# Squared key norms read from the gram's diagonal through DRAM, with every engine's list reordered

## Chip, cores and metric

One core of a Trainium2 chip runs the kernel. The metric is device time in microseconds (us) of one execution; a median over several executions is compared. TensorE (PE), VectorE (DVE), ScalarE (ACT), GpSimd (POOL) and SyncE (SP) each work through a list of their own, in order. SP only issues DMAs. "PEld" is PE's weight load and "SPq" is SP's queue of issues.

## What is computed

The input x is [8, 2048, 256]. The layer is attention with a gated delta rule, a layer norm, a feed-forward network (FFN) and a last layer norm. Cut to what matters:

```python
x_act = tanh(x); static_out = x_act @ W.T            # keys = queries = x_act, 16 heads of 16
# per head and token:  S = lam*S; u = beta*(v - S^T k); S += k u^T; o = S^T q
y = static_out + o
x1 = layernorm(x + layernorm(y)*gamma + ln_beta)
out = layernorm(x1 + (silu(x1 Wg^T) * (x1 Wu^T)) Wd^T)
```

As query and key are the same vector, the output of a token holds u times the key's squared norm. That norm, per token and head, is what the change touches.

## The kernel before

The sequence is cut into 32 steps of T = 64 tokens for all 8 batches, and a step into 4 windows of 16 tokens. A 128-row tile holds 8 batches x 16 tokens. Within a window the recurrence is solved in closed form. The state passes from window to window, so four such chains follow one another in each step and the steps follow each other. One window's chain is: PE `pe_keys_by_state` (keys times state), DVE and ACT form the rest R (`dve_rest_high`, `dve_rest_sum`, `act_rest`, `dve_rest_low`), PE `pe_inverse_by_rest` (the inverse of the window's triangular system times R), DVE and ACT form U (`act_update`, `dve_update_high`, `dve_update_low`), PE `pe_keys_by_update`, DVE and ACT form the new state S (`dve_state_high`, `dve_state_sum`, `act_state`, `dve_state_low`). All three products are L182.

Around it, software-pipelined by hand-written lists (`pe_step`, `dve_step`, `act_step`, `pool_step`, `sp_step`, one call of each per step; `live(s + k)` says for which neighbouring step a piece is done):

- Two steps ahead: SP loads x (`sp_load_x`, L994), ACT takes tanh of it in place in xa (L677), PE transposes the keys (L239), ACT and DVE split them into two float16 parts xt (L691, L406), SP stores xt to DRAM (`sp_store_keys`, L1003) and spreads it back to the block-diagonal e and the packed xb (L1016, L1025, 8 DMAs each).
- One step ahead: PE makes the gram matrices (`pe_gram`, L216), ACT and DVE add them up in gs (L715, L434), SP stores gs to DRAM and loads it back as gh with a (head, batch) pair in each partition (`sp_store_gram` L1033, `sp_load_gram` L1040), DVE multiplies by nmask (`dve_mask_gram`, L428), ACT copies it to tt (L721), and DVE inverts it in 28 operations (L443, L451). SP stores the inverse and loads tb (L1047, L1059), and loads kb, the keys as weights (L1072, 8 DMAs for each half step). A kb half may be loaded only when the window before that reads it last has ended (`sp` semaphore). PE's static output is L227 (`pe_static_out`).
- Norms: when k16 and the transposes have read xa, ACT squares it in place (`act_square`, L682) and DVE sums 16 columns each into nb (`dve_square_sums`, L418). The next x may be loaded only after that (`nr`). `dve_key_norms` (L423) scales nb, and POOL multiplies U by it (`pool_attention_out`, L915).
- Two steps behind: gate and up matmuls (L253), silu (L777), multiply (L495), split (L783, L953), down matmuls (L279), norms (L749, L757, L763) and the store.

SP waits at the head of a helper and then issues that helper's DMAs. Whatever stands behind a wait in its list is held up too.

Of the kernel before, what the change touches and what calls it, by code (L numbers as in the profile page):

```python
# [12 lines left out]
P = 128  # L13
# [3 lines left out]
NW = 4  # L17
# [18 lines left out]
def build(nc, x, W, ln_gamma, ln_beta, eta, lam_logit, w_gate, w_up, w_down, out):  # L36
# [3 lines left out]
    with ctx:  # L40
# [3 lines left out]
        def sem(name):  # L44
# [24 lines left out]
        nb = sb("nb", [P, 2, NW, H])  # L69
# [49 lines left out]
        scr_g = nc.dram_tensor("scr_g", [H, B, C, T], F32).ap()  # L119
        scr_t = nc.dram_tensor("scr_t", [2, H, B, C, T], F16).ap()  # L120
# [3 lines left out]
            sq=1, nr=1, nb=1, k16h=2, k16=2,  # L124
# [36 lines left out]
        FIRST, LAST = -3, NS + 3  # L161
# [122 lines left out]
        def pe_step(pe, s, p):  # L284
            if live(s - 2):
                pe_gate(pe, s - 2, p, 0)
                pe_up(pe, s - 2, p, 0)
                pe_gate(pe, s - 2, p, 1)
                pe_up(pe, s - 2, p, 1)
                pe_gate(pe, s - 2, p, 2)  # L290
                pe_up(pe, s - 2, p, 2)
                pe_gate(pe, s - 2, p, 3)
            if live(s):
                pe_keys_by_state(pe, s, p, 0)
            if live(s - 2):
                pe_gate(pe, s - 2, p, 4)
                pe_up(pe, s - 2, p, 3)
                pe_up(pe, s - 2, p, 4)
            if live(s + 1):
                pe_gram(pe, s + 1, 1 - p, 0, range(0, 8))  # L300
                pe_gram(pe, s + 1, 1 - p, 0, range(8, 16))
                pe_gram(pe, s + 1, 1 - p, 1, range(0, 8))
                pe_gram(pe, s + 1, 1 - p, 1, range(8, 16))
            if live(s - 2):
                pe_gate(pe, s - 2, p, 5)
            if live(s + 1):
                pe_gram(pe, s + 1, 1 - p, 2, range(0, 8))
                pe_gram(pe, s + 1, 1 - p, 2, range(8, 16))
            if live(s - 2):
                pe_up(pe, s - 2, p, 5)  # L310
                pe_down(pe, s - 2, p, 0, range(0, 4))
            if live(s + 1):
                pe_gram(pe, s + 1, 1 - p, 3, range(0, 8))
            if live(s):
                pe_inverse_by_rest(pe, s, p, 0)
            if live(s + 1):
                pe_gram(pe, s + 1, 1 - p, 3, range(8, 16))
            if live(s - 2):
                pe_down(pe, s - 2, p, 0, range(4, 6))
            if live(s):  # L320
                pe_keys_by_update(pe, s, p, 0)
            if live(s - 2):
                pe_down(pe, s - 2, p, 1, range(0, 3))
                pe_down(pe, s - 2, p, 1, range(3, 6))
            if live(s):
                pe_keys_by_state(pe, s, p, 1)
            if live(s + 1):
                pe_static_out(pe, s + 1, 1 - p, 0)
            if live(s):
                pe_inverse_by_rest(pe, s, p, 1)  # L330
            if live(s + 1):
                pe_static_out(pe, s + 1, 1 - p, 1)
            if live(s):
                pe_keys_by_update(pe, s, p, 1)
            if live(s + 1):
                pe_static_out(pe, s + 1, 1 - p, 2)
            if live(s):
                pe_keys_by_state(pe, s, p, 2)
            if live(s + 1):
                pe_static_out(pe, s + 1, 1 - p, 3)  # L340
            if live(s):
                pe_inverse_by_rest(pe, s, p, 2)
                pe_keys_by_update(pe, s, p, 2)
            if later(s + 2):
                pe_transpose_keys(pe, s + 2, p, 0)
                pe_transpose_keys(pe, s + 2, p, 1)
            if live(s):
                pe_keys_by_state(pe, s, p, 3)
                pe_inverse_by_rest(pe, s, p, 3)
            if live(s - 1):  # L350
                pe_transpose_x1(pe, s - 1, 1 - p, 0)
                pe_transpose_x1(pe, s - 1, 1 - p, 1)
            if live(s):
                pe_keys_by_update(pe, s, p, 3)
# [60 lines left out]
        def dve_square_sums(dve, q, p):  # L415
            dve.wait_ge(SEM["y1"], n_of("y1", q - 2))
            dve.wait_ge(SEM["sq"], n_of("sq", q))
            dve.tensor_reduce(nb[:, p, :, :], xa[:, :, :].rearrange("p n (h k) -> p n h k", h=H),  # L418
                              AX.X, ALU.add).then_inc(SEM["nr"], 1)

        def dve_key_norms(dve, q, p):
            dve.wait_ge(SEM["nr"], n_of("nr", q))
            dve.tensor_scalar(nb[:, p, :, :], nb[:, p, :, :], sc[:, BETAR:BETAR + 1], -0.5 / RS,  # L423
                              ALU.mult, ALU.add).then_inc(SEM["nb"], 1)
# [79 lines left out]
        def dve_step(dve, s, p):  # L504
            if live(s - 1):
                dve_state_sum(dve, s - 1, 1 - p, 3)
                dve_state_low(dve, s - 1, 1 - p, 3)
                dve_statistics(dve, s - 1, 1 - p, 1)
                dve_statistics(dve, s - 1, 1 - p, 2)
            if live(s + 1):  # L510
                dve_scale_keys(dve, s + 1, 1 - p, 0)
            if live(s - 2):
                dve_multiply(dve, s - 2, p, 1)
                dve_multiply(dve, s - 2, p, 2)
            if live(s):
                dve_key_norms(dve, s, p)
                dve_store_inverse(dve, s, p, 1)
            if live(s - 1):
                dve_statistics(dve, s - 1, 1 - p, 3)
            if live(s):  # L520
                dve_rest_high(dve, s, p, 0)
            if live(s - 1):
                dve_moments(dve, s - 1, 1 - p)
            if live(s - 2):
                dve_multiply(dve, s - 2, p, 3)
            if live(s + 1):
                dve_gram(dve, s + 1, 1 - p, 0)
            if live(s):
                dve_rest_sum(dve, s, p, 0)
            if live(s - 2):  # L530
                dve_multiply(dve, s - 2, p, 4)
            if live(s + 1):
                dve_gram(dve, s + 1, 1 - p, 1)
            if live(s - 1):
                dve_load_residual(dve, s - 1, 1 - p)
            if live(s - 2):
                dve_multiply(dve, s - 2, p, 5)
            if live(s):
                dve_rest_low(dve, s, p, 0)
            if live(s + 1):  # L540
                dve_gram(dve, s + 1, 1 - p, 2)
            if live(s):
                dve_update_high(dve, s, p, 0)
                dve_update_low(dve, s, p, 0)
            if live(s + 1):
                dve_gram(dve, s + 1, 1 - p, 3)
            if live(s - 2):
                dve_add_ffn(dve, s - 2, p, 0)
                dve_add_ffn(dve, s - 2, p, 1)
            if live(s - 1):  # L550
                dve_attention_norm(dve, s - 1, 1 - p, 0)
            if live(s):
                dve_state_high(dve, s, p, 0)
            if live(s - 1):
                dve_attention_norm(dve, s - 1, 1 - p, 1)
            if live(s):
                dve_state_sum(dve, s, p, 0)
            if live(s - 1):
                dve_attention_norm(dve, s - 1, 1 - p, 2)
            if live(s):  # L560
                dve_state_low(dve, s, p, 0)
            if live(s - 1):
                dve_attention_norm(dve, s - 1, 1 - p, 3)
            if live(s + 1):
                dve_scale_keys(dve, s + 1, 1 - p, 1)
            if live(s - 2):
                dve_add_ffn(dve, s - 2, p, 2)
                dve_add_ffn(dve, s - 2, p, 3)
            if live(s):
                dve_rest_high(dve, s, p, 1)  # L570
                dve_rest_sum(dve, s, p, 1)
                dve_rest_low(dve, s, p, 1)
            if live(s + 1):
                dve_square_sums(dve, s + 1, 1 - p)
            if live(s):
                dve_update_high(dve, s, p, 1)
                dve_update_low(dve, s, p, 1)
                dve_statistics(dve, s, p, 0)
                dve_state_high(dve, s, p, 1)
                dve_state_sum(dve, s, p, 1)  # L580
                dve_state_low(dve, s, p, 1)
            if live(s + 1):
                dve_mask_gram(dve, s + 1, 1 - p)
            if live(s):
                dve_rest_high(dve, s, p, 2)
                dve_rest_sum(dve, s, p, 2)
                dve_rest_low(dve, s, p, 2)
            if live(s + 1):
                dve_invert_scale(dve, s + 1, 1 - p, 1)
# [713 lines left out]
```

## Time and profile before

| | |
|---|---|
| median of 3 runs | 1710.55 us (1705.41 to 1717.15) |
| profiled execution | 1699.24 us, span 1697.4 us |
| PE / DVE / ACT / POOL busy | 80% / 80% / 66% / 50% |
| mean granted PE clock | 0.881 |
| DMA queue of SP | 52.1% of 16 engines, 701072 packets |

The profiled execution is one run, 11 us under the median of the others. Busy shares are averages over the whole span. A steady step lasts about 49 us, and in it the engines take turns at being late.

### The profile page before, as it was taken

How to read it: one execution, taken by the hardware profiler on the slowest of the kernel's cores; microseconds unless marked ns; L12 is line 12 of the kernel's file. 1: busy time of each engine (PE TensorE's matmuls, PEld its weight loads, DVE VectorE, ACT ScalarE, POOL GpSimd, SP SyncE). 2: the span in 40 equal slices, each digit the busy share in tenths (PEclk: the TensorE clock that was granted, in tenths of full speed). 3: DMA queues.
4: the chain of work that ended last, by engine and by line, in shares of the span. 5: the costliest groups of instructions: out<-in, count | busy, mean ns of one | idle time of the engine just before them, and what ended most of it. 6: DMA issues, size and time to landing. Idle time of an engine off the chain costs nothing.

```text
span 1697.4 us, 53741 instructions
## 1 busy us (share of the span) xinstructions
PE 1362.5 (80%) x21032; PEld 1062.5 (63%) x21032; DVE 1352.3 (80%) x3461; ACT 1115.9 (66%) x2357; POOL 842.8 (50%) x1106
## 2 busy tenths in 40 slices
PE   4357888888888888888888888887888888888764
PEld 3345676666666666666666666666666666666542
DVE  5588888888888888888888888888788788888841
ACT  3335777667767776676777677766667677676544
POOL 6124455555544655454455555445555544555542
PEclk9557889989989998898899899898999899899877
DMA  4556445565655555566455566654565555455200
GB/s 121 118 109 119 106 122 121 119 124 114 130 118 120 122 122 116 114 123 130 110 120 119 120 125 117 125 116 115 115 116 121 114 131 117 118 117 120 52 23 25
DMA packets 701325, 190.98 MB, mean 113 GB/s; under 512 B 620944, under 2 KB 688528, under 8 KB 701072
## 3 DMA queue, kind: packets, MB, share of 16 engines
q1 hardware_dynamic: 701072, 187.56, 52.1%
q8 instruction: 165, 2.70, 0.7%
q14 instruction: 88, 0.72, 0.1%
HBM read 103.55 MB, written 67.11 MB: 101 GB/s over the span
## 4 chain that ended last, share of the span: by engine, by line
DVE 29%; SPq 18%; PE 16%; DMA 13%; issue 12%; ACT 8%; POOL 4%; ACTq 0%; POOLq 0%; DVEq 0%
SPq L1059 8%; DMA xa<-L_attn_x 6%; PE pc L182 6%; DMA scr_g<-gs 5%; PE pg L253 4%; DVE tt L451 4%; SPq L1072 4%; PE pu L253 4%; DVE gs L443 3%; DVE gate L495 3%; SPq L994 3%; DVE xt L406 2%; DVE x1lo L488 2%; DVE U L382 2%; DVE R L377 2%
## 5 line engine op out<-in xcount | busy, mean ns | idle before, releaser
L953 POOL TENSOR_TENSOR hlo<-gate,hhi 128x512 f16<-128x512 f32 x192 | 264.0, 1385 | 357.0 <-ACT hhi L783 354.9
L182 PE MATMUL pc<-R,tb 128*128 128x32 f16 x4096 | 158.1, 186 | 119.3 <-DVE R L372 117.3
L182 PEld LDWEIGHTS pc<-R,tb 128*128 128x128 f16 x4096 | 146.7, 118 | 139.8 <-DVE R L372 137.7
L182 PE MATMUL pc<-U,kb 128*128 128x32 f16 x4096 | 158.9, 188 | 85.3 <-DVE U L382 85.1
L182 PEld LDWEIGHTS pc<-U,kb 128*128 128x128 f16 x4096 | 146.9, 118 | 114.7 <-DVE U L382 114.6
L182 PEld LDWEIGHTS pc<-S,e 128*128 128x128 f16 x4096 | 150.1, 118 | 67.9 <-DVE S L399 64.4
L182 PE MATMUL pc<-S,e 128*128 128x32 f16 x4096 | 157.1, 186 | 41.5 <-DVE S L399 41.4
L279 PE MATMUL pd<-wd_t,hhi 128*128 128x256 f16 x768 | 174.5, 274 | 7.5 <-POOL hlo L953 5.1
L279 PE MATMUL pd<-wd_t,hlo 128*128 128x256 f16 x768 | 174.1, 274 | 0.0
L216 PEld LDWEIGHTS pf<-xb,e 128*128 128x128 f16 x4096 | 153.8, 118 | 31.5 <-DMA e<-scr_x 16.3
L216 PE MATMUL pf<-xb,e 128*128 128x32 f16 x4096 | 156.3, 191 | 17.5 <-DMA e<-scr_x 15.9
L495 DVE SCALAR_TENSOR_TENSOR gate<-pu,gate 128x512 f32<-128x512 f32 x192 | 129.0, 685 | 48.0 <-ACT gate L777 35.1
L443 DVE TENSOR_TENSOR gs<-tt,gh 128x56 f32<-128x56 f32 (+6 forms) x448 | 145.2, 324 | 23.6 <-ACT tt L721 14.6
L253 PE MATMUL pg<-x1hi,wg_t 128*128 128x512 f16 x384 | 154.2, 402 | 11.5 <-DVE x1lo L488 10.0
L777 ACT ACTIVATE gate<-pg 128x512 f32<-128x512 f32 x192 | 113.7, 593 | 75.5 <-PE pg L253 71.8
L451 DVE TENSOR_TENSOR tt<-tt,gs 128x56 f32<-128x56 f32 (+6 forms) x448 | 146.4, 327 | 12.1
L783 ACT ACTIVATE hhi<-gate 128x512 f16<-128x512 f32 x192 | 119.7, 629 | 49.8 <-DVE gate L495 48.1
L253 PE MATMUL pg<-x1lo,wg_t 128*128 128x512 f16 x384 | 152.1, 396 | 0.0
L253 PE MATMUL pu<-x1lo,wu_t 128*128 128x512 f16 x384 | 149.0, 388 | 0.0
L253 PE MATMUL pu<-x1hi,wu_t 128*128 128x512 f16 x384 | 149.0, 388 | 0.0
L227 PE MATMUL pf<-w_t,xt 128*128 128x256 f16 x1024 | 139.4, 282 | 0.4 <-DVE gs L434 0.4
L434 DVE SCALAR_TENSOR_TENSOR gs<-pf,gs 128x256 f32<-128x256 f32 x128 | 85.0, 664 | 62.2 <-ACT gs L715 62.0
(132 smaller groups left out, 3222.4 us busy)
## 6 DMA issues: line engine op xcount, KB each, us to landing
xa<-L_attn_x SPq DMA_DIRECT2D x128, 128.0 KB
scr_x<-xt SPq DMA_DIRECT2D x64, 256.0 KB, 2.1
xb<-scr_x SPq DMA_DIRECT2D x256, 64.0 KB, 2.9
e<-scr_x SPq DMA_DIRECT2D x256, 64.0 KB, 3.7
scr_g<-gs SPq DMA_DIRECT2D x32, 512.0 KB, 3.5
gh<-scr_g SPq DMA_DIRECT2D x32, 512.0 KB, 3.3
kb<-k SPq DMA_DIRECT2D x512, 32.0 KB, 2.3
scr_t<-t SPq DMA_DIRECT2D x64, 256.0 KB, 3.6
```

The source lines that it names most:

```text
L182: last = pe.matmul(pc2[:, :, cols], stationary(h, a), moving[:, :, cols], start=a == 0, stop=a == 1)
L216: last = pe.matmul(pf[n % 2][:, 2 * h * C:2 * (h + 1) * C].rearrange("p (z j) -> p z j", z=2), E[p][:, ez, h, :, :, n].rearrange("p b i -> ...
L227: last = pe.matmul(pf[g][:, (n % 2) * D:(n % 2 + 1) * D], xt[:, half, xz, :, :, n].rearrange("p b i -> p (b i)"), w_t[:, half, wz, :], sta ...
L253: last = pe.matmul(bank[:, :], wt[:, half, t * P:(t + 1) * P], xp[:, half, :], start=half + part == 0, stop=half + part == 2)
L279: last = pe.matmul(pd[:, (n % 2) * D:(n % 2 + 1) * D], hp[:, t, n * P:(n + 1) * P], wd_t[:, t, :], start=n % 2 + t + part == 0, stop=n % 2 ...
L443: dve.tensor_tensor(tmp[:, m, 0:C - 1 - j, :], tt[:, m, j:j + 1, :].to_broadcast([P, j, C - 1 - j, NW]), gh[:, i, j, :][:, None].to_broadc ...
L451: dve.tensor_tensor(tt[:, m, i, :], tt[:, m, i, :], tmp[:, m, 0:C - 1 - j, :], ALU.add)\
L495: dve.scalar_tensor_tensor(gate[:, k, :], pu[k][:, :], W_SCALE * HS / XS, gate[:, k, :], ALU.mult, ALU.mult).then_inc(SEM["h"], 1)
L777: act.activation(gate[:, k, :], pg[k][:, :], ACT.Silu, scale=W_SCALE / XS).then_inc(SEM["si"], 1)
L783: act.activation(hhi[:, t, :], gate[:, t % 2, :], ACT.Copy).then_inc(SEM["hh"], 1)
L953: pool.tensor_tensor(hlo[:, t, :], gate[:, t % 2, :], hhi[:, t, :], ALU.subtract).then_inc(SEM["hl"], 1)
L1059: sp.dma_start(tb[C * b:C * (b + 1), g, :, b].rearrange("j h i z m -> j h (i z m)"), scr_t[g, :, b].rearrange("h j t -> j h t")).then_inc( ...
```

## The change

`act_square` and `dve_square_sums` go. The diagonal of the gram is the squared norm itself. nmask gets ones on its diagonal (it had zeros), so the masked gh keeps the norms there. SP writes this diagonal to a DRAM scratch, 16 bytes at a time, and reads it back with (batch, token) in the partitions. nb has four buffers by step and the layout [P, 4, H, NW]. The next x now waits for k16 in place of the sums. The helpers that issue 8 or 4 DMAs are cut into parts, so that the lists can interleave them, and all five lists are written anew.

```diff
-            sq=1, nr=1, nb=1, k16h=2, k16=2,
+            kd=16, nr=16, nb=1, k16h=2, k16=2,
...
-        def dve_square_sums(dve, q, p):
...
-        def act_square(act, q, p):
...
+                if z == 2:
+                    act.wait_ge(SEM["va3"], n_of("va3", q - 1))
...
             sp.wait_ge(SEM["tf"], n_of("tf", q - 1))
+            sp.sem_inc(s_hop, 1)
+            sp.wait_ge(SEM["kd"], n_of("kd", q - 1))
             sp.dma_start(gh[:, :, :, :].rearrange("p i j n -> p (i j n)"),
...
+        def sp_store_norms(sp, q, p):
+            sp.wait_ge(SEM["tf"], n_of("tf", q, 1))
+            sp.sem_inc(s_hop, 1)
+            sp.wait_ge(SEM["nr"], n_of("nr", q - 1))
+            sp.dma_start(scr_n.rearrange("h b i n -> (h b) i n"),
+                         gh[:, :, :, :].rearrange("p i j n -> p (i j) n")[:, 0:C * C:C + 1, :])\
+              .then_inc(SEM["kd"], 16)
+
+        def sp_load_norms(sp, q, p):
+            sp.wait_ge(SEM["kd"], n_of("kd", q))
+            sp.sem_inc(s_hop, 1)
+            sp.wait_ge(SEM["y1"], n_of("y1", q - 4))
+            sp.dma_start(nb[:, q % 4], scr_n.rearrange("h b i n -> (b i) h n")).then_inc(SEM["nr"], 16)
...
+            link(eng.memset(flat[:, 0:C * C:C + 1], 1.0))
```

The lists are rotated and reordered. Read in cyclic order, with the offset of the step behind the name, the pieces that changed their neighbours are these. SP before, from the store of the keys of step q = 0: store_keys 0 and 1, packed (8), spread (8), store_inverse 0 of -1, residual (4), store_inverse 1, load_inverse 0 (8), kb 1 (8), store_gram, load_gram, load_inverse 1 (8), x of +1 (4), store_out (4), kb 0 (8). SP after:

```text
store_keys 0, 1;  packed 2, spread 2, packed 6, spread 6;  store_inverse 0;  residual 4;
load_inverse 0 (8);  kb 1 (4);  store_inverse 1;  kb 1 (4);  store_gram;
load_inverse 1 (4);  x (2);  load_inverse 1 (4);  load_gram;  x (2);
kb 0 (2);  STORE_NORMS;  kb 0 (2);  store_out 4;  LOAD_NORMS;  kb 0 (4)
```

- PE: `pe_up(4)` stands behind the first two grams, where it stood ahead of them. `pe_inverse_by_rest(0)` stands ahead of both halves of gram 3. Static outputs 0 and 1 both follow `pe_keys_by_state(1)`, 2 follows `pe_inverse_by_rest(1)`, 3 follows `pe_inverse_by_rest(2)`. They stood one each behind keys 1, inverse 1, update 1 and keys 2.
- DVE: `dve_scale_keys(0)` and `dve_store_inverse(1)` move into the stretch of the grams, the latter to behind gram 2. `dve_statistics(0)` and `dve_invert_scale(3)` move by one or a few places, the latter to ahead of `dve_update_low(2)`.
- ACT: `act_decay(2)` moves to behind the variances, `act_rest(3)` ahead of all four `act_first_norm`, which had two ahead of it. `act_hidden(1)` stands ahead of `act_store_inverse(0)`.
- POOL keeps its cyclic order.

## Rows read from the trace of the kernel before

**Rows 1.** The page's busy times, its chain, and the tile gh.

```profile
PE 1362.5 (80%) x21032; PEld 1062.5 (63%) x21032; DVE 1352.3 (80%) x3461; ACT 1115.9 (66%) x2357; POOL 842.8 (50%) x1106
...
DVE 29%; SPq 18%; PE 16%; DMA 13%; issue 12%; ACT 8%; POOL 4%; ACTq 0%; POOLq 0%; DVEq 0%
...
L428 DVE TENSOR_TENSOR gh<-gh,nmask x32: 1216/1218/1225, 47.7 to 1565.3; 128x1024 f32<-128x1024 f32 x32
```

**Rows 2.** Waits, all engines: us in total, times, longest us.

```profile
ACT xa L677 <- DMA xa<-L_attn_x: 18.7, 20, 2.0
```

**Rows 3.** Timeline of PE and ACT in three steps: start us, us, what.

```profile
819.01 1.04 PE L227 MATMUL pf<-w_t,xt 128*128 128x256 f16 x8
842.41 0.61 PE L253 MATMUL pg<-x1hi,wg_t 128*128 128x512 f16 x1 [0.24 <-DVE x1lo L488]
...
1161.59 1.04 PE L227 MATMUL pf<-w_t,xt 128*128 128x256 f16 x8
1174.70 1.06 ACT L677 ACTIVATE xa<-xa 128x1024 f32<-128x1024 f32 x1 [1.96 <-DMA xa<-L_attn_x]
1187.48 0.61 PE L253 MATMUL pg<-x1hi,wg_t 128*128 128x512 f16 x1 [0.24 <-DVE x1lo L488]
```

**Rows 4.** Waits of SP's queue.

```profile
SPq L1038 <- DMA scr_g<-gs: 104.5, 32, 4.5
SPq L998 <- DVE xt L406: 58.9, 63, 4.4
SPq L1025 <- DMA scr_x<-xt: 56.3, 32, 4.3
```

**Rows 5.** Timeline of SP's queue, one step.

```profile
814.69 0.39 SPq L1033 DMA_DIRECT2D scr_g<-gs  x1
818.55 0.34 SPq L1040 DMA_DIRECT2D gh<-scr_g  x1
819.01 3.81 SPq L1059 DMA_DIRECT2D tb<-scr_t  x8
822.93 2.66 SPq L994 DMA_DIRECT2D xa<-L_attn_x  x4
825.71 2.68 SPq L1090 DMA_DIRECT2D y_out<-xr  x4
828.51 6.17 SPq L1072 DMA_DIRECT2D kb<-k  x8
835.66 1.20 SPq L1003 DMA_DIRECT2D scr_x<-xt  x2
...
843.06 4.92 SPq L1016 DMA_DIRECT2D e<-scr_x  x8
```

**Rows 6.** Timeline of DVE, ACT and POOL around the removed operations.

```profile
820.82 1.21 DVE L418 TENSOR_REDUCE nb<-xa 128x64 f32<-128x1024 f32 x1
822.65 0.42 DVE L377 SCALAR_TENSOR_TENSOR R<-pc,U 128x256 f32<-128x256 f32 x1 [0.62 <-ACT U L664]
...
818.49 1.06 ACT L682 ACTIVATE xa<-xa 128x1024 f32<-128x1024 f32 x1 [0.51 <-DVE k L412]
...
819.22 0.20 POOL L928 TENSOR_TENSOR nq<-sm,by_16d 128x4 f32<-128x4 f32 x1 [4.25 <-DVE xr L501]
```

**Rows 7.** Timeline of DVE and ACT: scale keys, mask, an inversion piece, two first norms.

```profile
817.68 0.78 DVE L412 SCALAR_TENSOR_TENSOR k<-xa,kcol,k 128x512 f16<-128x512 f32 x1
826.26 1.22 DVE L428 TENSOR_TENSOR gh<-gh,nmask 128x1024 f32<-128x1024 f32 x1
831.78 0.30 DVE L443 TENSOR_TENSOR gs<-tt,gh 128x144 f32<-128x144 f32 x1
...
837.12 1.08 ACT L757 ACTIVATE xr<-res,nm,rs 128x256 f32<-128x256 f32 x2
```

**Rows 8.** DMA issues of the page: KB each, median us to landing.

```profile
e<-scr_x SPq DMA_DIRECT2D x256, 64.0 KB, 3.7
...
gh<-scr_g SPq DMA_DIRECT2D x32, 512.0 KB, 3.3
```

**Rows 9.** The DMA view of 814 to 819 us, where the gram store runs alone.

```profile
scr_g<-gs SPq DMA_DIRECT2D x1, 512.0 KB, 3.8
```

**Rows 10.** Timeline of PE: the first gram of that step.

```profile
854.12 2.06 PE L216 MATMUL pf<-xb,e 128*128 128x32 f16 x57
```

**Rows 11.** Windows of 4 us at the start of two steps' gate matmuls: busy, granted clock.

```profile
842.50:846.50 4.00, 4.00 (x10) 1.40 (x11) 3.15 (x11) 1.94 (x3) 0.00 (x0) 0.50 0.59 94
1387.50:1391.50 4.00, 4.00 (x20) 1.80 (x19) 3.57 (x11) 2.42 (x4) 0.00 (x0) 1.00 0.77 122
```

More of the change, by code:

```diff
@@ new lines, in pe_step @@
+            if live(s + 3):
+                pe_keys_by_state(pe, s + 3, 1 - p, 0)
+            if live(s + 1):
+                pe_gate(pe, s + 1, 1 - p, 4)
+                pe_up(pe, s + 1, 1 - p, 3)
+            if live(s + 4):
+                pe_gram(pe, s + 4, p, 0, range(0, 8))
+                pe_gram(pe, s + 4, p, 0, range(8, 16))
+                pe_gram(pe, s + 4, p, 1, range(0, 8))
+                pe_gram(pe, s + 4, p, 1, range(8, 16))
+            if live(s + 1):
+                pe_up(pe, s + 1, 1 - p, 4)
+                pe_gate(pe, s + 1, 1 - p, 5)
@@ new lines, in dve_step @@
+            if live(s + 1):
+                dve_update_high(dve, s + 1, 1 - p, 2)
+            if live(s + 2):
+                dve_invert_scale(dve, s + 2, p, 3)
+            if live(s + 1):
+                dve_update_low(dve, s + 1, 1 - p, 2)
+            if live(s + 2):
+                dve_invert_add(dve, s + 2, p, 3)
+                dve_invert_scale(dve, s + 2, p, 4)
+                dve_invert_add(dve, s + 2, p, 4)
+            if live(s + 1):
+                dve_state_high(dve, s + 1, 1 - p, 2)
+                dve_state_sum(dve, s + 1, 1 - p, 2)
@@ new lines, in dve_step @@
+            if live(s + 2):
+                dve_invert_scale(dve, s + 2, p, 5)
+            if live(s + 1):
+                dve_state_low(dve, s + 1, 1 - p, 2)
+            if later(s + 3):
+                dve_transpose_keys(dve, s + 3, 1 - p, 0)
+            if live(s + 2):
+                dve_invert_add(dve, s + 2, p, 5)
+            if later(s + 3):
+                dve_transpose_keys(dve, s + 3, 1 - p, 1)
+            if live(s + 1):
+                dve_rest_high(dve, s + 1, 1 - p, 3)
+                dve_rest_sum(dve, s + 1, 1 - p, 3)
@@ new lines, in dve_step @@
+            if live(s + 2):
+                dve_invert_scale(dve, s + 2, p, 9)
+            if live(s + 1):
+                dve_update_low(dve, s + 1, 1 - p, 3)
+            if live(s + 2):
+                dve_invert_add(dve, s + 2, p, 9)
+            if live(s):
+                dve_transpose_x1(dve, s, p, 0)
+                dve_transpose_x1(dve, s, p, 1)
+            if live(s + 2):
+                dve_invert_scale(dve, s + 2, p, 10)
+                dve_invert_add(dve, s + 2, p, 10)
+                dve_invert_scale(dve, s + 2, p, 11)
+                dve_invert_add(dve, s + 2, p, 11)
+                dve_invert_scale(dve, s + 2, p, 12)
+                dve_invert_add(dve, s + 2, p, 12)
+                dve_invert_scale(dve, s + 2, p, 13)
+                dve_invert_add(dve, s + 2, p, 13)
+                dve_invert_scale(dve, s + 2, p, 14)
+                dve_invert_add(dve, s + 2, p, 14)
@@ new lines, in dve_step @@
+            if live(s + 2):
+                dve_state_low(dve, s + 2, p, 0)
+            if live(s + 1):
+                dve_attention_norm(dve, s + 1, 1 - p, 2)
+            if live(s + 3):
+                dve_scale_keys(dve, s + 3, 1 - p, 1)
+            if live(s):
+                dve_add_ffn(dve, s, p, 2)
+                dve_add_ffn(dve, s, p, 3)
+            if live(s + 1):
+                dve_attention_norm(dve, s + 1, 1 - p, 3)
+            if live(s + 2):
+                dve_rest_high(dve, s + 2, p, 1)
+                dve_rest_sum(dve, s + 2, p, 1)
+                dve_rest_low(dve, s + 2, p, 1)
+                dve_update_high(dve, s + 2, p, 1)
+                dve_update_low(dve, s + 2, p, 1)
+                dve_state_high(dve, s + 2, p, 1)
+                dve_state_sum(dve, s + 2, p, 1)
+                dve_state_low(dve, s + 2, p, 1)
@@ new lines, in act_step @@
+            if live(s + 1):
+                act_state(act, s + 1, 1 - p, 3)
+            if live(s + 2):
+                act_store_inverse(act, s + 2, p, 1)
+            if live(s):
+                act_hidden(act, s, p, 2)
+                act_multiply(act, s, p, 1)
+                act_multiply(act, s, p, 2)
+                act_hidden(act, s, p, 3)
+            if live(s + 2):
+                act_rest(act, s + 2, p, 0)
+            if live(s + 3):
+                act_gram(act, s + 3, 1 - p, 0)
@@ new lines, in act_step @@
+            if live(s + 2):
+                act_update(act, s + 2, p, 0)
+            if live(s + 3):
+                act_gram(act, s + 3, 1 - p, 3)
+            if live(s + 2):
+                act_state(act, s + 2, p, 0)
+            if live(s + 3):
+                act_scale_keys(act, s + 3, 1 - p, 1)
+            if live(s + 2):
+                act_decay(act, s + 2, p, 1)
+            if live(s):
+                act_variance(act, s, p, 3, 0)
+            if live(s + 2):
+                act_rest(act, s + 2, p, 1)
@@ L825, in act_step @@
+            if live(s + 2):
+                act_state(act, s + 2, p, 1)
+            if live(s):
+                act_last_norm(act, s, p, 3)
+            if live(s + 2):
+                act_rest(act, s + 2, p, 2)
+            if live(s + 3):
+                act_mask_gram(act, s + 3, 1 - p)
+            if later(s + 4):
+                act_activate(act, s + 4, p)
+            if live(s + 2):
+                act_update(act, s + 2, p, 2)
             if live(s + 1):
-                act_scale_keys(act, s + 1, 1 - p, 1)
@@ new lines, in act_step @@
+            if live(s + 2):
+                act_state(act, s + 2, p, 2)
+            if later(s + 4):
+                act_transpose_keys(act, s + 4, p, 0)
+                act_transpose_keys(act, s + 4, p, 1)
+            if live(s + 2):
+                act_rest(act, s + 2, p, 3)
+            if live(s + 1):
+                act_first_norm(act, s + 1, 1 - p, 0)
+                act_first_norm(act, s + 1, 1 - p, 1)
+                act_first_norm(act, s + 1, 1 - p, 2)
+                act_first_norm(act, s + 1, 1 - p, 3)
@@ L1108, in sp_step @@
[L1108 to L1116 removed]
+            if live(s + 3):
+                sp_load_inverse(sp, s + 3, 1 - p, 1, range(0, 2))
+                sp_load_inverse(sp, s + 3, 1 - p, 1, range(2, 4))
@@ new lines, in sp_step @@
+            if later(s + 5):
+                sp_load_x(sp, s + 5, 1 - p, range(0, 2))
+            if live(s + 3):
+                sp_load_inverse(sp, s + 3, 1 - p, 1, range(4, 6))
+                sp_load_inverse(sp, s + 3, 1 - p, 1, range(6, 8))
+            if live(s + 4):
+                sp_load_gram(sp, s + 4, p)
+            if later(s + 5):
+                sp_load_x(sp, s + 5, 1 - p, range(2, 4))
+            if live(s + 4):
+                sp_load_kb(sp, s + 4, p, 0, range(0, 2))
+                sp_store_norms(sp, s + 4, p)
+                sp_load_kb(sp, s + 4, p, 0, range(2, 4))
@@ L1164, in _ @@
             sp_store_keys(eng, 0, 0, 1)
[L1165 to L1166 removed]
+            sp_spread_packed_keys(eng, 0, 0, range(B))
+            sp_spread_keys(eng, 0, 0, range(B))
             all_steps(eng, sp_step)
```

690 lines of the change are left out of this document (288 added, 402 removed).

## The prediction

> **What bounds the kernel now.** I read the page first. PE and DVE are both busy 80% and neither fills the span, while the chain that ended last passes through SP's queue for 18% and DMA for 13% [rows 1]. So the lists' order and SP matter more than any engine's sum. The mask operation comes 32 times between 47.7 and 1565.3 us [rows 1], so a steady step is (1565.3 - 47.7) / 31 = 48.95 us. The other 180 us are start and end.
>
> The timeline splits a step in two [rows 3]. The FFN part runs from the first gate matmul to the first static output, and PE has work without a gap in it. The chain part runs from there to the next gate matmul. It is three windows of the recurrence in sequence, PE waits again and again for DVE, and only latency counts. The chain part is 842.41 - 819.01 = 23.40 us in one step and 1187.48 - 1161.59 = 25.89 us in another. In the second, ACT's tanh waited 1.96 us for x, and `act_update(2)`, which the chain needs, stands right behind it [rows 3]. The tanh waits 18.7 us in total, in 20 steps [rows 2], and as those two steps suggest, nearly all of it lengthens the chain.
>
> Why x is late is to be seen in SP's list. The x loads stand behind `sp_load_gram`, and this behind the gram store's landing: 104.5 us of waiting in 32 steps, 3.27 each [rows 4]. In the step shown the store is issued at 814.69, the load at 818.55, and x is out only at 822.93 + 2.66 = 825.59 [rows 5].
>
> **What the change takes away.** The reduce is 1.21 us and ends near 822.03. DVE then idles 0.62 us until ACT's U lets it go on at 822.65 [rows 6]. It lies in a gap longer than itself: worth 0 on the path, 32 x 1.21 = 39 us if the gap were not there. The square is 1.06 us from 818.49. The variance that stands next on ACT needs POOL's mean, which starts at 819.22 [rows 6], so ACT would have waited to about 819.4 anyway: worth 0 too, at most 0.1 us a step. What hides both is the latency of the chain part, and the change doesn't remove that.
>
> The wait on the gram store goes from in front of x. In the new SP list a store_gram at 814.69 is followed by four tb loads (half of 3.81 us), two x loads (half of 2.66), four tb, load_gram and two x [rows 5]. The x load now also needs `dve_scale_keys(1)`, done at 817.68 + 0.78 = 818.46 [rows 7], so x is out at 818.46 + 1.33 + 1.91 + 0.34 + 1.33 = 823.4 in place of 825.6. The longest wait was 2.0 us [rows 2], so all of it goes: -18.7 us. This is the only sure gain. Behind it is the copy of gh on ACT, which was already the limit in the steps without a wait.
>
> **What it adds and moves.** Four places become tighter.
>
> First, gh. It is issued at 818.46 + 1.33 + 1.91 = 821.7 and lands 3.3 us later [rows 8], at 825.0, where before it landed by 818.55 + 3.3 = 821.9. The mask wants it at 826.26 [rows 7], with 1.2 us to spare. A gh behind tb and x in the DMA engines may take longer than 3.3, for it ran nearly alone before. I take 0.05 us a step, 2 us in all; with 1 us more landing and jitter it would be up to 0.5 a step, 15 us.
>
> Second, the norms. `sp_store_norms` waits for the mask's end, 826.26 + 1.22 = 827.48 [rows 7]. Queued behind it on SP are six kb loads, four output stores, the norm load, and then the store of the next keys. No such issue is in the trace. The nearest are the gram store and load, 0.39 and 0.34 us [rows 5], and a kb load, 6.17 / 8 = 0.77; I take 0.5, nearer to the former, as they move as many packets. The sum is 827.48 + 0.5 + 2 x 0.77 + 2.68 + 0.5 + 4 x 0.77 = 835.8. Before, SP came to the key store at 835.66 [rows 5] after waiting for DVE's xt, as it does nearly every step (58.9 us [rows 4]). So SP arrives just in time, and its slack there is spent. At 0.77 each it is 0.7 us late. The landing of the norm store is covered by two kb and four output issues, 1.54 + 2.68 = 4.2 us. The gram store, of 128 x 16 = 2048 pieces as well, landed in 3.8 us when it ran alone [rows 9], with 256 bytes a piece instead of 16. I take this as the value; a landing at 2 us changes nothing, and one over 4.2 pushes SP. Who waits for the norms themselves is POOL a step later, which costs nothing.
>
> The Trainium skill ("DMA: Bandwidth & Descriptors", Specifications) says that transfers under 512 bytes make the DMA engine read, modify and write. It speaks against this change: 16-byte pieces written to DRAM. The trace has no such piece; its 256-byte ones fall under the same rule, and by that 3.8 us already contains it. If a 16-byte write cost twice as much the landing would pass the 4.2 us, which is a rival below.
>
> Third, e before the gram. The last of the e loads is issued at 843.06 + 4.92 = 847.98 and lands 3.7 us later [rows 8], at 851.7. PE starts the gram at 854.12 [rows 10]. That step began with the half clock; with the full one the same FFN work is about 2 us shorter, as 4 us held 10 matmuls at the clock 0.50 and 20 at 1.00 [rows 11]. The gram then comes at 852.1, and moving `pe_up(4)`, four matmuls of 4.00 / 20 = 0.2 us, behind it brings it to 851.3: earlier than e. So PE waits about 0.4 us in the steps with a full clock, somewhat more if SP is late, and not in the others. I take 0.2 a step, 6 us.
>
> Fourth, the chain part. `dve_invert_scale(3)`, 0.30 us [rows 7], now delays `dve_update_low(2)` by some 0.2 us. Two first norms of 1.08 us together [rows 7] stand behind `act_rest(3)`, so x1 is whole later and its transposes, by my count, 0.25 us. Two static outputs in a row after keys 1 take 2.08 us [rows 3], about what PE idled and worked there before. Together between 0 and 0.6 us, of which later gaps take back some; I take 0.25 a step, 8 us. The FFN part holds the same matmuls and stays as it is.
>
> The two new DMAs add 4096 packets a step to 701072 / 32 = 21,900. SP's queue is at 52% of the DMA engines; it stays below what would hold up more than single transfers. I put nothing on it, and let the bounds above stand for it. One more memset in the setup is nothing.
>
> The sum against the profiled execution: -18.7 + 2 + 6 + 8 = -3 us, 1699.24 to 1696. As a share, -0.16%. On the median of 1710.55 that is 1708 us. (A measurement of this kernel can tell about 1% from no change, 17 us.) The forecast's own range, with each added term at its ends, is 1692 to 1723.
>
> **Rivals.** (A) The gain stays whole. The tighter places keep their margin, the moves in the chain part fall in gaps, and the lateness of SP that also delays kb and the scale of the keys in a few steps goes: -19 to -25 us, 1688. For it speaks that every margin computed above is near zero, and not below. Chance 0.24.
>
> (B) SP becomes the bound. The norm store lands later than its cover of 4.2 us, or the two issues cost well above 0.5, so that key store, e and the gram come late each step. It decides from SP arriving 0.5 us after xt, beyond which PE waits at the first gram microsecond for microsecond. With a landing of twice the time over a fixed 2 us, 2 + 2 x 1.8 = 5.6 us, SP is 1.5 us late: 31 x 1.5 - 18.7 = +28, 1738. The Trainium skill's rule on writes under 512 bytes, named above, would lead here. For it: SP's slack at the key store was the only one left. Against it: x and gram no longer queue behind a landing, and 3.27 us a step of waiting are free. Chance 0.20.
>
> (C) The clock. PE's matmuls in the chain part get sparser in windows 1 to 2, since static outputs 2 and 3 leave them. If the granted clock then falls in each step up to the gate matmuls, as in the step with 10 matmuls in 4 us [rows 11], about half of the steps lose 2 us more: +31 to +45 less 18.7, about 1735. If it falls less, the gain is of like size. Chance 0.07 for slower.
>
> (D) The change doesn't do what it says: gh's lateness takes x's place, and the tanh waits behind the mask instead. 1712. Chance 0.04.
>
> **How the numbers follow.** The forecast has 0.45, and it lies within 1% for most of its range; A gives most of faster, B and C slower, and D is no change. Faster by over 1% is 0.25, within 1% 0.47, slower 0.28. The range takes in A's centre and B's: 1682 to 1742.
>
> **What would show it.** ACT's wait of the tanh for x should be gone, and SP's wait for the landing of the gram store too; DVE's busy time falls by 39 us and ACT's by 34 without the step following. SP's wait for xt shrinks from 58.9 us towards 0. PE should show a wait for e at the first gram, in steps with a full clock. I am wrong if the step falls below 48.3 us, or if the first gram or the mask waits for DMA by over 1 us a step, or if the low clock covers clearly more or less of the gate matmuls.

## The result and the profile after

| | before | after |
|---|---|---|
| median | 1709.13 us (1705.41 to 1717.15, 4 runs) | 1897.09 us (1894.20 to 1905.69, 4 runs) |
| profiled span | 1697.4 us | 1892.4 us |
| granted PE clock | 0.881 | 0.820 |

The ratio is 1.110, interval 1.105 to 1.115: the change costs 188 us, and my range ended at 1742. On the page the order of the engines is the same, each is busy for a smaller share, and the operations that were taken out are gone (ACT 1115.9 to 1064.1 us busy, [rows 1]). DVE's sum rose a little all the same (1352.3 to 1360.8), as its residual addition and its scaling of the norms took longer (last section).

```profile
PE 1401.1 (74%) x21032; PEld 1074.0 (57%) x21032; DVE 1360.8 (72%) x3430; ACT 1064.1 (56%) x2325; POOL 819.7 (43%) x1106
...
q1 hardware_dynamic: 833168, 189.66, 51.6%
```

The second line is the queue: 132,096 packets more than before, and yet no larger share of the DMA engines. Bandwidth is not what ran out. The tile gh gives the step: its mask operations now run from 47.0 to 1754.0 us, (1754.0 - 47.0) / 31 = 55.06 us against 48.95 [rows 1], and 31 x 6.1 = 189 us is the whole loss.

```profile
L422 DVE TENSOR_TENSOR gh<-gh,nmask x32: 1216/1221/1226, 47.0 to 1754.0; 128x1024 f32<-128x1024 f32 x32
```

The waits of SP's queue (us in total, times, longest) answer to [rows 4]:

```profile
SPq L1045 <- DMA scr_n<-gh: 112.8, 27, 7.2
SPq L1015 <- DMA scr_x<-xt: 65.3, 32, 4.9
SPq L1037 <- DVE gh L422: 42.2, 30, 2.9
...
SPq L986 <- DVE xt L406: 2.9, 2, 2.6
```

The wait for the gram store (104.5 us) is gone, and one for the norm store has come in its place, 112.8 us. There is a new wait for the mask, 42.2. The wait for xt has fallen from 58.9 to 2.9 us: SP used to be early at the key store and now is late. Who suffers is in the waits of PE:

```profile
PE pf L217 <- DMA e<-scr_x: 94.2, 31, 22.7
```

31 of the 32 first grams wait for e, and in the steady part (the 23 steps between the 5th and the 28th mask) it is 2.1 us in every step. The tanh's wait for x [rows 2] is no longer among the waits. One step of SP's queue, the counterpart of [rows 5]:

```profile
812.33 0.59 SPq L1039 DMA_DIRECT2D scr_n<-gh  x1
812.96 1.65 SPq L1080 DMA_DIRECT2D kb<-k  x2
814.73 3.81 SPq L1099 DMA_DIRECT2D y_out<-xr  x4
822.57 0.40 SPq L1047 DMA_DIRECT2D nb<-scr_n  x1
823.01 3.86 SPq L1080 DMA_DIRECT2D kb<-k  x4
827.06 0.97 SPq L991 DMA_DIRECT2D scr_x<-xt  x2
```

The norm store is issued at 812.33 and the load that waits for it at 822.57. The other issues cover it up to 818.54, and then SP stands for 4.0 us with kb, the key store and e behind it. Over all 32 steps store and load are 9.7 us apart (8.6 to 10.5). For 32 KB this is two and a half times the 3.8 us in which the gram store landed its 512 KB [rows 9]. The issues in between have grown too: four output stores take 3.81 us, where it was 2.68 [rows 5], and in the mean of the steady part 3.7 against 2.7.

In the steady part SP spends 42.2 us of a step in its DMA issues (37.6 before), 3.7 in the short gaps between them (under 0.3 us each) and 9.5 in longer ones, its waits (8.3 before). That makes 55.4, the length of a step there (49.2 before). Such a sum comes out for any queue that works in order, so it doesn't show who sets the pace. That is for e1 below, where nothing but SP's list differs.

### The profile page after: what moved, and what is told of

The parts are those of the page before. It is cut to its first block and busy times, and to the rows that moved or that the text cites. A ratio compares the mean times of both kernels' runs of the same rounds, so it can differ in the third digit from the quotient of the medians.

```text
span 1892.4 us, 53806 instructions
## 1 busy us (share of the span) xinstructions
PE 1401.1 (74%) x21032; PEld 1074.0 (57%) x21032; DVE 1360.8 (72%) x3430; ACT 1064.1 (56%) x2325; POOL 819.7 (43%) x1106
## 3 DMA queue, kind: packets, MB, share of 16 engines
q1 hardware_dynamic: 833168, 189.66, 51.6%
## 5 line engine op out<-in xcount | busy, mean ns | idle before, releaser
L940 POOL TENSOR_TENSOR hlo<-gate,hhi 128x512 f16<-128x512 f32 x192 | 239.7, 1256 | 567.3 <-ACT hhi L771 567.2
L183 PEld LDWEIGHTS pc<-U,kb 128*128 128x128 f16 x4096 | 152.4, 118 | 49.9 <-DVE U L382 47.3
L254 PE MATMUL pg<-x1hi,wg_t 128*128 128x512 f16 x384 | 158.5, 413 | 13.3 <-DVE x1lo L482 12.7
L228 PE MATMUL pf<-w_t,xt 128*128 128x256 f16 x1024 | 160.1, 316 | 0.2 <-DVE gs L428 0.2
L701 ACT ACTIVATE gs<-pf 128x256 f32<-128x256 f32 x128 | 83.9, 655 | 127.0 <-PE pf L217 126.7
L254 PE MATMUL pu<-x1hi,wu_t 128*128 128x512 f16 x384 | 153.9, 401 | 0.0
L254 PE MATMUL pu<-x1lo,wu_t 128*128 128x512 f16 x384 | 153.7, 400 | 0.0
```

The costliest lines, as they stand in the source:

```text
L183: last = pe.matmul(pc2[:, :, cols], stationary(h, a), moving[:, :, cols], start=a == 0, stop=a == 1)
L228: last = pe.matmul(pf[g][:, (n % 2) * D:(n % 2 + 1) * D], xt[:, half, xz, :, :, n].rearrange("p b i -> p (b i)"), w_t[:, half, wz, :], sta ...
L254: last = pe.matmul(bank[:, :], wt[:, half, t * P:(t + 1) * P], xp[:, half, :], start=half + part == 0, stop=half + part == 2)
L701: act.activation(gs[:, :, :, n], pf[n % 2][:, :].rearrange("p (h z j) -> p z h j", h=H, z=2)[:, 0], ACT.Copy, scale=1.0 / (KS * KS)).then_ ...
L940: pool.tensor_tensor(hlo[:, t, :], gate[:, t % 2, :], hhi[:, t, :], ALU.subtract).then_inc(SEM["hl"], 1)
```

## Experiments

All times are medians; ratios are to the kernel before on the same chip. "Issues" is the time that SP spends in DMA issues per step, waits left out, in the steady part. "Store to load" is the mean time from the norm store's issue to the load's, and "landing" the median time from the store's issue to its landing, where the trace has it. In the changed kernel and in p32 the load waits for the landing in nearly every step, and store to load stands for it.

| kernel | time, us | ratio (interval) | issues | store to load | landing |
|---|---|---|---|---|---|
| before | 1709 to 1712 | 1 | 37.6 | | |
| b1 no square, old lists | 1712.8 | 1.001 (0.999 to 1.003) | 37.7 | | |
| e2 new lists, no norm DMAs | 1704.0 | 0.996 (0.994 to 0.998) | 38.4 | | |
| m1 the same, with the wait for the mask | 1704.7 | 0.997 (0.994 to 0.999) | 38.7 | | |
| e3 compact store | 1767.9 | 1.034 (1.030 to 1.038) | 40.8 | 4.3 | 1.5 |
| p64 slots of 64 bytes (first run 1782.0) | 1778.0 | 1.041 (1.037 to 1.044) | 41.5 | 5.5 | 5.3 |
| p512 slots of 512 bytes | 1778.3, one run | | 41.5 | 5.2 | 4.1 |
| s64 full pieces of 64 bytes | 1771.9, one run | | 41.7 | 5.1 | 3.3 |
| p32 slots of 32 bytes | 1840.0, one run | | 41.4 | 7.2 | |
| after | 1897.1 | 1.110 (1.105 to 1.115) | 42.2 | 9.7 | |
| e1 norm load later | 1809.0 | 1.058 (1.053 to 1.063) | 42.3 | covered | |
| v1 compact, other places | 1814.5 | 1.060 (1.058 to 1.063) | 39.9 | covered | 1.8 |
| v2 as v1, 16-byte pieces | 1922.5 | 1.124 (1.121 to 1.127) | 44.1 | covered | |
| v3 compact, load behind e | 1744.7 | 1.022 (1.019 to 1.025) | 41.0 | covered | 1.8 |
| v4 as v3, later scaling | 1746.3 | 1.021 (1.018 to 1.025) | 41.0 | covered | 1.8 |
| v5 compact, both in slack | 1713.7 | 1.001 (0.998 to 1.003) | 39.7 | 3.5 | 2.9 |
| v6 64-byte slots, in slack | 1768.9 | 1.031 (1.027 to 1.035) | 41.7 | 6.0 | 5.8 |

**e1: the norm load later.** T1 held that the wait blocks SP, T2 that the pieces slow down the other transfers, T3 that the lists are slow.

```diff
                 sp_spread_packed_keys(sp, s + 5, 1 - p, range(6, 8))
+            if live(s + 4):
+                sp_load_norms(sp, s + 4, p)     # was ahead of kb 0, range(4, 6)
```

> The norm load moves in SP's list from ahead of the last four kb loads to behind the last packed keys load, some 10 us of other issues later. Nothing else changes. Theory T1 (the wait for the norm store's landing blocks SP, and the key store, e and the first gram behind it): the wait is covered, the step falls from 55.1 to about 49.5 us and the time to 1700 to 1740. Rival T2 (the 16-byte pieces load the DMA engines and slow down every other transfer, wherever the wait stands): the time stays above 1840. Rival T3 (the new lists are slow by themselves): it stays near 1890.

1809: neither. The wait is fully covered and 88 us come back, although nothing but SP's list was touched. So SP set the pace, and about half of the loss was SP standing there. The other 98 us stay. The queue shows what remains, here in one of the worse steps:

```profile
832.54 0.58 SPq L1039 DMA_DIRECT2D scr_n<-gh  x1
833.16 1.58 SPq L1080 DMA_DIRECT2D kb<-k  x2
834.86 5.05 SPq L1099 DMA_DIRECT2D y_out<-xr  x4
```

The issues behind the norm store are held up, 5.05 us for four in place of 2.68. In the mean of the steady part it is 3.4 for the four output stores, where e2 below has 2.7, and 3.8 for the four kb loads behind them, where e2 has 2.9. SP is slowed by the pieces even where it doesn't wait for them. A part of the 98 us is of the experiment's own making: with the later load DVE waits 14.6 us for the norms, for which it doesn't wait in the changed kernel.

**e2, b1: the lists and the passes alone.** e2 drops both norm DMAs and the semaphore waits on them; b1 drops square and sums from the old lists and lets x wait for k16, as the change does. nb is zero in both.

```diff
-                sp_store_norms(sp, s + 4, p)
-                sp_load_norms(sp, s + 4, p)
+            link(eng.memset(nb[:, :, :, :], 0.0))
```

> The new lists with neither norm store nor norm load; nb is filled with zeros once, so the output lacks the norm term. T1 and T2: 1680 to 1715, that is what the lists are worth without the norm transfers. T3: near 1890.

> The kernel before with its lists, without the square pass and the sums; nb is filled with zeros once, so the output lacks the norm term. As predicted both lie in gaps: within 0.5% of before, 1700 to 1712. If they were on the path (2.3 us a step), 1640.

e2 is 1704.0 and b1 1712.8, both as expected. T3 has fallen. The new lists are 0.4% better than the old ones, and the square and the sums cost nothing in the old lists. In e2 SP is early at the key store again, 91.5 us in all or 2.9 a step:

```profile
SPq L985 <- DVE xt L406: 91.5, 63, 6.2
```

**e3: one contiguous store.**

```diff
+            dve.tensor_copy(nd[:, :, :], gh[:, :, :, :].rearrange("p i j n -> p (i j) n")[:, 0:C * C:C + 1, :])
...
-            sp.dma_start(scr_n.rearrange("h b i n -> (h b) i n"),
+            sp.dma_start(scr_n.rearrange("h b i n -> (h b) (i n)"), nd[:, :, :].rearrange("p i n -> p (i n)"))
```

> DVE copies the diagonal of gh into a small tile (128x64, about 0.25 us a step, behind the third window's first operation), and the norm store moves that tile, 256 contiguous bytes a partition in place of 16 pieces of 16 bytes. List positions as in the changed kernel. If the landing of 10 us comes from the number or the size of the pieces written, it falls to 2 to 4 us, and T1 and T2 give 1695 to 1730. If it comes from something else about this transfer (its place among kb and output), the landing stays near 10 us and the time near 1890.

The landing is no longer waited for at all, and 129 us come back. But 1768 misses the 1695 to 1730 that both theories gave.

```profile
SPq L1047 <- DVE nd L430: 64.7, 32, 2.7
...
SPq L996 <- DVE xt L407: 6.4, 6, 2.0
```

SP waits 2.0 us a step for the small tile, and has again no slack left at the key store. The landing is short, 1.5 us:

```profile
scr_n<-nd SPq DMA_DIRECT2D x32, 32.0 KB, 1.5
```

The traces of e3 and e2 also say where most of the other 64 us lie. In the steady part a step of e3 is 2.4 us longer (51.5 against 49.0). SP waits 2.0 us for the tile, spends 0.75 in the two norm issues, and four kb loads right behind the norm load take 4.4 us in place of 2.9. Of these 4.3 us the slack ahead of the key store took 2.2, and 2.1 are left. The load, too, is of 2048 pieces of 16 bytes, and it too holds up the issues behind it.

**p64, p32, p512, s64: what is slow in the 16-byte store.** Only the pitch in DRAM changes (and in s64 the piece).

```diff
-        scr_n = nc.dram_tensor("scr_n", [H, B, C, NW], F32).ap()
+        scr_n = nc.dram_tensor("scr_n", [H, B, C, 16], F32).ap()[:, :, :, 0:NW]   # 8 in p32, 128 in p512
```

> The changed kernel, with each 16-byte piece written at the head of a 64-byte slot of its own in DRAM (the array is four times as long). The time from norm store to norm load was 9.7 us in the changed kernel. If several pieces written to the same 64 bytes of DRAM hinder each other, it falls to 4 to 6 us; if the price is by the piece, whatever its neighbours, it stays at 9 to 10.5 us.

> The changed kernel, with 2048 pieces of 64 bytes in the norm store, in place of 16, each filling a 64-byte slot (the pieces are taken from the first columns of gh and not from the diagonal, so the output's norm term is another). If the price is that of pieces smaller than 64 bytes, the time from norm store to norm load falls from 9.7 to 4 to 5 us, as for the 256-byte pieces of the gram store; if it is a price of any piece under 256 bytes or of this place in the list, it stays at 9 to 10.5 us.

> The padded kernel with an interval: 1775 to 1790, ratio 1.037 to 1.046, 110 to 120 us below the changed kernel, whose only difference is that four pieces share 64 bytes of DRAM.

> The changed kernel with each 16-byte piece in a 32-byte slot of DRAM, so that two share 64 bytes. If sharing 64 bytes is the cause, the time from norm store to norm load lies between 5.4 (none shares) and 9.7 us (four share), near 6 to 8. If 32 bytes are the unit, it falls to 5.4 already.

> Each 16-byte piece in a slot of 512 bytes. If the read, modify and write of the page's rule works on units up to 512 bytes, the time from norm store to norm load falls clearly below 5.4 us, to the 4.2 to 4.6 us that the list's own issues take; if 64 bytes is the unit, it stays at 5.0 to 5.8 us.

Four pieces to 64 bytes: 9.7 us from store to load. Two: 7.2. One: 5.5. Slots of 512 bytes give 5.2 and full pieces of 64 bytes 5.1, but there the landing is no longer what counts: two kb loads and four output stores are issued in between, and they alone take about 5 us. The landings themselves go on falling. Here are p64 (second run), p512 and s64:

```profile
scr_n<-gh SPq DMA_DIRECT2D x32, 32.0 KB, 5.3
...
scr_n<-gh SPq DMA_DIRECT2D x32, 32.0 KB, 4.1
...
scr_n<-gh SPq DMA_DIRECT2D x32, 128.0 KB, 3.3
```

In p512 none of the 32 stores took over 4.4 us, and in p64 none under 4.6, in either run. The number of pieces, their size in SBUF and the list are the same for all four slots. So the slow part is how close together the small pieces lie in DRAM. Moving them apart to 64 bytes is worth 1897 - 1778 = 119 us, and moving them further still shortens the landing by 1.2 us, for which this kernel has no use. (The expectation for p512 took store to load as its sign, which the issues in between keep near 5 us whatever the landing; it could not tell.) Whether 64 bytes is a unit of its own is not shown: a bound at which the price stops falling was not found. And 64 bytes filled by one piece land sooner than 64 bytes with a quarter of them written. The wait in p64, first run, is down to a rest:

```profile
SPq L1045 <- DMA scr_n<-gh: 14.5, 18, 3.4
```

**v1, v2: store in the hole behind the key store.** In v1 POOL makes the copy; v2 stores from gh and has none. In both the load stands ahead of the second store of the inverse, and DVE scales the norms behind the residual.

```diff
                 sp_store_keys(sp, s + 5, 1 - p, 1)
+                sp_store_norms(sp, s + 4, p)
...
+                sp_load_norms(sp, s + 4, p)
                 sp_store_inverse(sp, s + 4, p, 1)
...
                 dve_load_residual(dve, s + 1, 1 - p)
+                dve_key_norms(dve, s + 2, p)
```

> The changed kernel, with the diagonal copied to a small tile by POOL where POOL idles (a 128x64 copy, about 0.3 us), the norm store of 256 contiguous bytes a partition issued right behind the key store, where SP waits 2 us for a landing anyway, the norm load issued before the second store of the inverse, where SP waits for DVE anyway, and the scaling of the norms on DVE moved behind the residual. Theory T1 (what costs is SP being held up ahead of the key store, by waits and issue time): the time is that of the lists without norm transfers, 1700 to 1712, ratio 0.993 to 1.001. Rival T2 (the transfers themselves load the DMA engines): with 128 pieces for the store and 2048 for the load it stays above by some of the 64 us that the compact store at the old position cost, 1715 to 1740.

> As the previous kernel, but the store takes the 16-byte pieces from gh as in the change. No wait of SP depends on its landing now before some 20 us have gone. T1: equal to the compact one, 1700 to 1712. T2 (the pieces hold up the transfers behind them): e and xb come behind it in the DMA engines, so their issues and landings grow by 4 us or more a step and the first gram waits: 1800 to 1860.

v1 missed for a reason of my own making, which DVE's timeline shows:

```profile
812.43 2.20 DVE L458 TENSOR_TENSOR res<-res,lnb 128x1024 f32<-128x1024 f32 x1
814.93 1.96 DVE L418 TENSOR_SCALAR nb<-nb,sc 128x64 f32<-128x64 f32 x1 [0.30 <-DMA nb<-scr_n]
816.81 0.41 DVE L378 SCALAR_TENSOR_TENSOR R<-pc,U 128x256 f32<-128x256 f32 x1
```

The scaling stands right ahead of the recurrence's update, waits for the load (38.0 us in all), and takes 1.96 us itself. v1 alone tells nothing of T1. The pair tells of T2: v2 is 108 us slower with the same lists but for POOL's copy, with eight packed loads at 8.4 us of issue in place of 4.6 (means of the steady part), and PE waits 99.8 us for e in place of 17.1. The 16-byte pieces hold up the queue behind them at this place too.

**v3, v4: the load behind e, the scaling moved twice.** The load goes ahead of the first store of the inverse. The scaling stands behind the last statistics (v3) or the second gram addition (v4).

> As v1 (POOL's compact copy, the store behind the key store where SP waits for a landing anyway), but the norm load is issued ahead of the first store of the inverse, where SP waits for DVE, and DVE scales the norms behind the last statistics of the step before, some 4 us after that, away from the recurrence. The same transfers as in the compact kernel at the change's positions, which took 1768. T1 (the wait for the mask and the waits and issues ahead of the key store are the price): back to the lists without norms, 1698 to 1712. T2 (the transfers load the DMA engines): 1725 to 1770 again.

> As v3, only DVE's scaling of the norms stands behind the second gram addition, some 4 us later, where DVE waits for PE anyway. In v3 DVE waited 33.6 us there for the norm load, of 41 us by which v3 is above the lists without norms. If that wait is the rest of the price: 1700 to 1715. If the transfers' load on the queue is: 1730 to 1745 as v3.

1745 and 1746. DVE's wait of 33.6 us for the norms in v3 is gone in v4, and the time is the same, so that wait was not the rest, as I had thought. What both share is the queue behind the norm load, here in v4:

```profile
871.29 0.42 SPq L1055 DMA_DIRECT2D nb<-scr_n  x1
871.83 1.33 SPq L1061 DMA_DIRECT2D scr_t<-t  x1
873.21 2.67 SPq L1099 DMA_DIRECT2D res<-L_attn_x  x4
876.00 5.26 SPq L1074 DMA_DIRECT2D tb<-scr_t  x8
```

The store of the inverse right behind the norm load takes 1.33 us here and 1.7 in the mean, where it is 0.4 in e2. The 5.26 us of tb are not a sign of it: in the mean of the steady part this group takes 4.5 us in v4 and in e2 alike. But norm load and held-up store put tb and kb about 2 us further back in the queue, and they come late: PE waits 19.0 us for tb and ACT 31.5 for kb, where it is 5.0 and 5.5 in e2.

```profile
ACT k L687 <- DMA kb<-k: 31.5, 26, 2.3
...
PE pc L184 <- DMA tb<-scr_t: 19.0, 18, 3.8
```

**m1: the wait for the mask alone.**

```diff
                 sp_load_kb(sp, s + 4, p, 0, range(0, 2))
+                sp.wait_ge(SEM["tf"], n_of("tf", s + 4, 1))
```

> The new lists without norm store and norm load, nb zero as before, but SP still waits for the mask at the place where the norm store stood, behind the first two kb loads. It prices that wait alone. SP waited 2 us a step there in the compact kernel and had 2.9 us of slack at the key store without norms: if slack covers it, 1700 to 1712; if it passes through to the first gram, 1720 to 1760, and then it is a main part of the 64 us between the lists alone and the compact kernel.

1704.7 against 1704.0: the wait lies in SP's slack. SP waits 41.4 us for the mask, and its wait for xt falls from 91.5 to 43.8.

**v5, v6: both norm DMAs in SP's slack.** The store stands behind the output stores, when the copy is long done, and the load behind the last kb loads, right ahead of SP's wait for xt.

```diff
                 sp_store_out(sp, s + 1, 1 - p, range(3, 4))
+                sp_store_norms(sp, s + 4, p)
                 sp_load_kb(sp, s + 4, p, 0, range(4, 6))
                 sp_load_kb(sp, s + 4, p, 0, range(6, 8))
+                sp_load_norms(sp, s + 4, p)
```

> The compact kernel with store and load both in the slack that SP has ahead of the key store (2.8 us a step in the lists without norms): the store behind the output stores, where the mask and POOL's copy are long done, the load behind the last kb loads, right before SP waits for DVE's xt. The same transfers as in v3, v4 and the compact kernel. If the price of the compact ones is the place where SP's queue is held up (T1, by issues and by the back-pressure behind the load's 2048 pieces): 1700 to 1722. If it is the load of the transfers wherever they stand (T2): 1740 to 1750 like v3 and v4.

> The same places, with the 16-byte pieces straight from gh, each in a 64-byte slot. The store lands after 3.8 us or more, and kb issues of 2.7 us cover it, so SP waits 1 to 2 us for it, and the slack is then used up: 1715 to 1755 under T1, 1760 to 1790 under T2.

v5 is 1713.7, the same as before. Its transfers are those of e3, v3 and v4, which took 31 to 54 us more, so for the compact form the place decides and not the load as such (in e3 DVE makes the copy in place of POOL; v3 and v4 differ from v5 by nothing but places):

```profile
836.45 0.40 SPq L1046 DMA_DIRECT2D scr_n<-nd  x1
836.89 2.65 SPq L1087 DMA_DIRECT2D kb<-k  x4
839.66 1.36 SPq L1054 DMA_DIRECT2D nb<-scr_n  x1
841.73 1.15 SPq L998 DMA_DIRECT2D scr_x<-xt  x2
```

The issues cover the store's landing, and behind the load SP was going to wait anyway: of the 91.5 us for xt there are 34.1 left.

```profile
SPq L993 <- DVE xt L407: 34.1, 53, 1.6
```

v6 is 1769. It puts the 2048 padded pieces in the same places and lies inside of what T2 gave and outside of T1's. SP waits 30.0 us for the store, the four kb loads behind it take 4.4 us of issue against 2.8 in v5, and its step in the steady part is 51.3 us against 49.2. With 2048 pieces both ways the slack of 2.9 us didn't hold them in either of the two places tried.

## Why the prediction was wrong

**The step that failed** is "I take this as the value": the norm store's landing at 3.8 us, taken from the gram store because it has as many pieces. It was 9.7 us or a little less. The gram store's pieces are 256 bytes; the norm store packs four pieces into each 64 bytes, and the same 2048 pieces with more room between them landed in 7.2, 5.3 and 4.1 us. So the number of pieces was the wrong thing to go by. I even wrote, of the Trainium skill's rule on writes under 512 bytes ("DMA: Bandwidth & Descriptors", Specifications), that 3.8 us "already contains it". The rule as it stands doesn't tell the two apart: s64's pieces of 64 bytes are under 512 as well, and 2048 of them landed in 3.3 us. It would have warned of the direction, and I gave the rival that it led to 5.6 us and a chance of 0.20.

**A second step that failed**: "I put nothing on it" for the 4096 packets more. Their share of the DMA engines is indeed small (51.6% against 52.1%). But behind such a transfer SP's next issues take longer: output stores by 1.0 us in the mean, packed loads by nearly 4 in v2, and kb loads behind the norm load by 1.6 in e3. e1 without any wait for the landing is still 105 us above e2, with 42.3 us of issues a step against 38.4.

**What was right.** Rival B named the chain, and the trace shows it link by link: landing beyond the cover (4.2 us in the forecast, about 5 measured), SP late at the key store, e late, PE waiting at the first gram. Its price of 1.5 us a step was for a landing of 5.6 us; p64, whose store landed in 5.3, is 68 us above before, and B gave 28. It left out the held-up issues. The two issues themselves were sized rightly, 0.59 and 0.40 us. The tanh's wait went as forecast. Square and sums were worth 0, shown by b1. The lists without the norm DMAs were forecast at -3 us with +6 us of e waits in it; e2 measures -7, in which PE waits for e only in 2 of 23 steps. The slack at the key store was 2.9 us and not the near zero that I computed from one step with both norm issues; it carried the mask's wait (m1) and the compact transfers (v5). ACT's busy time fell, by 52 us; DVE's was to fall by 39 and rose by 8.5.

**The other rivals.** C, the clock: it did fall, to 0.820, but e2 has the same order on PE and 0.864 at 1704 us. The lower clock came with PE's waits for e and doesn't start the loss. It may add to it: PE's busy time rose from 1362.5 to 1401.1 us for the same matmuls, and how much of the 188 us that is was not separated. D, gh: DVE waits for it 11 times, 13.5 us in all (2 were forecast, 15 the bound), and the tanh doesn't wait behind it.

**The sum, shown by runs:** new lists 1704; two norm DMAs with one contiguous store at the change's places 1768; 2048 padded pieces 1778; four pieces sharing 64 bytes 1897. Of the 64 us of the second step, the wait for the mask is nothing by itself (m1), and together with the two issues and the kb loads held up behind the norm load it overruns the slack of 2.9 us. These parts are read from the traces of e2 and e3, and no run takes the last one away alone. No version that has the norms beats the kernel before: v5 equals it, and what it saves on ACT and DVE was never on the path.

## To carry to other kernels

Price a small transfer by how its pieces fall in DRAM and not by their number: gather a strided diagonal into a contiguous tile first (here a landing of 1.5 us in place of 9.7), or at least give each piece 64 bytes of its own (5.3). When one queue issues everything, find where it is early and where it is late, and put a new transfer, the hold-up behind it included, where the queue would have waited. Removing work that lies in gaps gives nothing, so anything added for it must be free too.

## What was not expected of the hardware

- 2048 pieces of 16 bytes written to DRAM: 9.7 us from issue to landing with four pieces in 64 bytes, 7.2 with two, 5.3 with one, 4.1 with one in 512. 2048 full pieces of 64 bytes took 3.3, and the same 32 KB from a contiguous tile 1.5. Reading the 2048 packed pieces back took 3.2 us (median to landing).
- SP's issues behind such a store are held up: eight 64 KB loads took 8.4 us of issue in v2 against 4.6 in v1. Behind a load of 2048 such pieces it is less: four kb loads 4.4 us in e3 against 2.9 in e2.
- DVE's scaling of 128x64 took a median of 244 ns before, 668 ns after, 1517 ns in v1 and 248 ns in v4. In the step of v1 shown POOL was working on v and gamma at that time (3.33 us). With the new lists that operation took a median of 3.37 us against 2.40 before, and DVE's residual addition beside it 2.21 against 1.37. The two seem to hold each other up; no run separates it.
